# Feed-forward experts ahead of multi-query attention: last slots with tokens stationary, scatters ahead of gathers, first queries' parts moved up

## The chip, the cores and the metric

The kernel runs on one core of one Trainium2 chip. The metric is the device time of one execution in microseconds. A core has five engines with queues of their own: PE (TensorE; PEld is its weight load), DVE (VectorE), ACT (ScalarE), POOL (GpSimd) and SP (SyncE, which here only issues DMAs). They meet through semaphores written out by hand.

## What is computed

Two layers over x of 8 sequences x 512 tokens x 128 channels: linear attention, a mixture of experts, multi-query attention, a filter, each with a layer norm in front and a residual. The change lies in the experts and in the passage to the attention behind them:

```python
capacity = max(1, int(Sz * CAP_FACTOR / E) + 1)          # 512 * 2 / 8 + 1 = 129
scores = softmax(einsum('bsd,ed->bse', x, router_w))
gate_vals, sel_idx = top_k(swapaxes(scores, 1, 2), capacity)
tokens = x[b_idx, sel_idx]
h = gelu(einsum('becd,edh->bech', tokens, w1) + b1)
y = einsum('bech,ehd->becd', h, w2) + b2
out = zeros_like(x).at[b_idx, sel_idx].add(y * gate_vals[..., None])
```

Each of the 8 experts takes 129 tokens of each sequence. 128 of them fill a tile of 128 partitions; the 129th, the "last slot", makes 64 rows in all (8 sequences x 8 experts), which go a way of their own.

## The kernel before, in words

The experts run in 16 phases p (`PHASES`, L985). Phases 0 to 7 are experts 0 to 7 on sequences 0 to 3 (`FIRST`), phases 8 to 15 the same experts on sequences 4 to 7 (`SECOND`). In a phase the four sequences' 128 rows are gathered by POOL with four indirect DMAs (`pool_moe_gathers`, L1040, into one of four buffers of x_row), transposed on PE (`pe_moe_xT`, L1262), copied by ACT, multiplied by w1 in four chunks (`pe_moe_hidden`, L1270, with ACT's Gelu behind each), multiplied by w2 (`pe_moe_output`, L1278) and given bias and gate on DVE (`dve_moe_gated`, L1073, into one of two buffers of yg). The result is added into x. For sequence 0 (`BY_PE`) PE does this with a matmul against a 0/1 mask (`pe_moe_scatter`, L1288). For the others POOL issues an accumulating indirect DMA into x_dram (`pool_moe_scatter`, L1033): three per phase in the first half, four in the second. SP writes x to x_dram before (`x_to_dram`) and reads it back after (`x_from_dram`).

Each engine's order is written out by hand. PE goes through places (p, i), i = 0 to 3 (`moe_pe`, L1356): the hidden chunk i of phase p + 1; at i = 0 the transposes of phase p + 2; a share of the attention's first score maxima (from p = 10 on); `pe_moe_side` (L1330), which holds everything else; output i of phase p. DVE's order is `moe_dve` (L1172), ACT's `moe_act` (L1250), POOL's `moe_pool` (L1049). POOL first gathers phases 0 to 3, and then for each p: the gathers for phase p + 4, a wait for the gated rows of p (m_y), the scatters of p. Bias and gate of phase p wait until the scatters of p - 2 have landed; the gathers for phase n wait until the transposes of n - 4 are done.

The last slots use one bank of PSUM ("side") in stages at fixed phases (`LAST_AT`, L1010): transpose of the 64 gathered rows (p = 1), hidden layer with the weights stationary and 8 columns moving (p = 2, L1317), output likewise (p = 4, L1323), transpose back (p = 5, L1326). Then `pe_moe_rest` (L1298) spreads them over the tokens, one sequence per place of phases 6 and 7, 64 rows deep (L1300). ACT keeps the result for sequences 1 to 3, DVE adds it into x for 4 to 7, and for sequence 0 PE adds it to the sums.

The passage: when the first half is done, sequence 0 gets its layer norm (statistics on DVE, L305, L310; square root and normalising on ACT), its queries (L2057) and keys (L2064), in the side work of phases 8 to 11. The queries are split into three bf16 parts (`dve_q_parts`, L1690; the first part on ACT), and SP writes these with 18 DMAs per sequence into qT. Sequences 1 to 3 come back from x_dram, get the rest added (L1138) and their statistics, ahead of the split. The attention's maxima, its shift rows (SP, L2024) and its first scores end the passage; POOL's causal masking (L1872) of the attention is queued behind POOL's last scatter.

Of the kernel before, what the change touches and what calls it, by code (L numbers as in the profile page):

```python
# [21 lines left out]
P = 128  # L22
# [26 lines left out]
def build(nc, x_in, w_qkv, w_out, router_w, w1, b1, w2, b2, w_attn, w_proj, wf_re, wf_im, f_bias,  # L49
# [18 lines left out]
    with ExitStack() as ctx:  # L68
# [743 lines left out]
        new_stage()  # L812
        rmax = scratch("rmax", [P, B * NT])
# [30 lines left out]
        place = scratch("place", [P, 2, T])  # L844
# [136 lines left out]
        FIRST, SECOND = tuple(range(G)), tuple(range(G, B))  # L981
        BY_PE, DMA_FIRST, DMA_SECOND = FIRST[:1], FIRST[1:], SECOND
        BY_DMA = DMA_FIRST + DMA_SECOND
        SEQ = FIRST + SECOND
# [7 lines left out]
        m_full, m_taken = count("side_bank_filled"), count("side_bank_emptied")  # L992
# [6 lines left out]
        side = bank[0]  # L999
# [3 lines left out]
        def placed_no(e, b):  # L1003
# [5 lines left out]
        LAST_XT, LAST_HIDDEN, LAST_OUTPUT, LAST_T = range(4)  # L1009
        LAST_AT = {1: LAST_XT, 2: LAST_HIDDEN, 4: LAST_OUTPUT, 5: LAST_T}  # L1010
        REST_AT = dict(zip(((6, 0), (6, 1), (6, 2), (6, 3), (7, 0), (7, 1), (7, 2)), BY_DMA))
        REST_SUM_AT = dict(zip(((7, 3),), BY_PE))
        fill_no = {key: n + 1 for n, key in enumerate([("last", n) for n in LAST_AT.values()]
                                                      + [("rest", b) for b in BY_DMA])}

# [32 lines left out]

        def moe_pool(pool):  # L1049
# [9 lines left out]
            for p in range(PHASES):  # L1059
                if p + 4 < PHASES:  # L1060
# [39 lines left out]
        def dve_moe_add_sums(dve, b):  # L1100
            dve.wait_ge(m_placed, placed_no(E - 1, b))
            nc.vector.tensor_tensor(x_sb[:, b], x_sb[:, b], sums[b][:, :].rearrange("p (k d) -> p k d", d=D),
                                    ALU.add).then_inc(m_added, 1)

        def dve_moe_last(dve, stage_no):
            by_seq = seqmask[0:BE, :].unsqueeze(2).broadcast_to([BE, B, D])
            dve.wait_ge(m_full, fill_no["last", stage_no])
# [1249 lines left out]
```

## Time and profile before

| | us |
|---|---|
| median of 3 runs | 752.31 |
| lowest and highest | 749.36, 752.98 |
| the profiled execution's own time | 752.71 |
| its span, first to last instruction | 751.0 |
| PE busy | 618.1 (82%) |
| DVE busy | 521.4 (69%) |
| POOL busy | 391.2 (52%) |
| ACT busy | 374.9 (50%) |

Rows of the trace give a start in us, a duration, an engine, a line of the kernel, an operation and what it writes and reads; [..] is the engine's idle time just before, and what ended it. The experts' phases run from about 250 to 434 us of the span, the attention's eight turns follow. An f32 matmul shows as two PE instructions. Matmuls are pipelined, so their durations overlap; the chain of waits gives them without the overlap.

### The profile page before, as it was taken

How to read it: one execution, taken by the hardware profiler on the slowest of the kernel's cores; microseconds unless marked ns; L12 is line 12 of the kernel's file. 1: busy time of each engine (PE TensorE's matmuls, PEld its weight loads, DVE VectorE, ACT ScalarE, POOL GpSimd, SP SyncE). 2: the span in 40 equal slices, each digit the busy share in tenths (PEclk: the TensorE clock that was granted, in tenths of full speed). 3: DMA queues.
4: the chain of work that ended last, by engine and by line, in shares of the span. 5: the costliest groups of instructions: out<-in, count | busy, mean ns of one | idle time of the engine just before them, and what ended most of it. 6: DMA issues, size and time to landing. Idle time of an engine off the chain costs nothing.

```text
span 751.0 us, 14209 instructions
## 1 busy us (share of the span) xinstructions
PE 618.1 (82%) x4111; PEld 369.9 (49%) x4111; DVE 521.4 (69%) x1779; ACT 374.9 (50%) x800; POOL 391.2 (52%) x529
## 2 busy tenths in 40 slices
PE   2478888888405999999799778999999999999894
PEld 1235555554302688776566533545454545444453
DVE  8458888887794112225478859898989898987554
ACT  0322333331450423326622357777777777767873
POOL 0077777776004777776887554343434343433341
PEclk9989999999855999999999989999999999999997
DMA  9400000000040122244663244040304030200011
GB/s 297 133 0 1 1 0 0 0 1 0 16 140 28 49 43 39 39 93 84 110 98 35 26 82 53 10 59 10 59 10 60 9 60 9 60 5 2 24 52 42
DMA packets 45145, 34.55 MB, mean 46 GB/s; under 512 B 4304, under 2 KB 41728, under 8 KB 45072
## 3 DMA queue, kind: packets, MB, share of 16 engines
q1 hardware_dynamic: 33584, 25.15, 14.5%
q0 software_dynamic: 10144, 7.90, 7.5%
q10 hardware_dynamic: 1344, 0.62, 0.3%
q8 instruction: 34, 0.56, 0.3%
q14 instruction: 39, 0.32, 0.2%
HBM read 14.13 MB, written 9.70 MB: 32 GB/s over the span
## 4 chain that ended last, share of the span: by engine, by line
PE 46%; DVE 16%; issue 8%; ACT 4%; POOL 1%; DMA 1%; DVEq 0%; ACTq 0%; POOLq 0%
PE bank L2146 8%; PE wide L1275 6%; DVE masked L1744 6%; PE wide L2133 5%; PE wide L2082 5%; PE wide L1283 4%; PE bank L1283 4%; PE bank L2082 2%; PE wide L2158 2%; ACT L282 1%; DVE mx L1744 1%; DVE slot_t L886 1%; POOL x_row L1045 1%; PE bank L2057 1%; PE bank L1300 1%
## 5 line engine op out<-in xcount | busy, mean ns | idle before, releaser
L1941 ACT ACTIVATE pexp<-wide 128x512 f32<-128x512 f32 (+2 forms) x384 | 180.9, 536 | 77.9 <-PE wide L2133 75.9
L1744 DVE CUSTOM_DVE_ANT_0 masked<-wide,mask_qk 128x128 f32<-128x128 f32 (+3 forms) x423 | 182.8, 477 | 46.9 <-PE wide L2082 46.1
L1872 POOL TENSOR_SCALAR_AFFINE_SELECT pexp<-pexp 128x256 f32<-128x256 f32 x256 | 106.4, 429 | 166.7 <-ACT pexp L1941 165.2
L2133 PE MATMUL wide<-qT,kTe 128*128 128x256 bf16 (+3 forms) x512 | 121.8, 301 | 6.1 <-ACT pexp L1941 3.7
L2082 PE MATMUL wide<-kTm,qT 128*128 128x128 bf16 (+3 forms) x423 | 102.6, 300 | 13.2 <-DVE mx L1744 10.8
L1036 POOL DMA_INDIRECT x_dram<-yg,row_u x56 | 89.4, 1597 | 30.6 <-DVE yg L1088 15.7
L1225 ACT ACTIVATE hT<-wide,b1T 128x512 f32<-128x512 f32 x64 | 43.9, 686 | 100.7 <-PE wide L1275 100.7
L1045 POOL DMA_INDIRECT x_row<-xln_dram,row_u x64 | 62.6, 978 | 52.5 <-DVE slot_tok L915 33.6
L2146 PE MATMUL bank<-pexp,vx 128*32 128x512 f32 (+3 forms) x1024 | 85.4, 446 | 4.9 <-POOL pexp L1872 4.9
L2133 PEld LDWEIGHTS wide<-qT,kTe 128*128 128x128 bf16 x512 | 48.6, 99 | 42.5 <-ACT pexp L1941 23.1
L1275 PE MATMUL wide<-xgT,w_sb 128*128 128x512 f32 x128 | 67.4, 612 | 1.5 <-ACT xgT L1218 1.5
L2082 PEld LDWEIGHTS wide<-kTm,qT 128*128 128x128 bf16 x423 | 35.7, 97 | 65.8 <-DVE mx L1744 48.3
L615 POOL TENSOR_TENSOR kv<-kx,qv 128x1024 f32<-128x1024 f32 x32 | 62.0, 1949 | 1.1 <-PE wide L718 1.1
L2146 PEld LDWEIGHTS bank<-pexp,vx 128*32 128x32 f32 x1024 | 26.2, 110 | 45.5 <-issue 27.7
L1744 DVE CUSTOM_DVE_ANT_0 masked<-bank,mask_qk 128x256 f32<-128x256 f32 (+3 forms) x89 | 45.5, 528 | 4.0 <-PE bank L2082 4.0
L409 DVE TENSOR_TENSOR prod<-wide,qs 128x1024 f32<-128x1024 f32 x26 | 31.7, 1224 | 21.3 <-PE wide L718 20.2
L717 PE MATMUL wide<-kv,cst 128*128 128x512 f32 x64 | 35.9, 645 | 11.5 <-DVE prod L409 5.6
L1744 DVE DVE_READ_ACCUMULATOR2_ANT mx<- 128x1 f32 x512 | 42.5, 83 | 0.0
L421 DVE TENSOR_REDUCE y_in<-prod 128x128 f32<-128x1024 f32 x32 | 38.2, 1213 | 1.3 <-PE bank L741 0.6
L1283 PE MATMUL wide<-w_sb,hT 128*128 128x128 f32 x256 | 34.9, 280 | 0.0
L1283 PEld LDWEIGHTS wide<-w_sb,hT 128*128 128x128 f32 x256 | 32.1, 192 | 5.2 <-issue 4.3
L1283 PE MATMUL bank<-w_sb,hT 128*128 128x128 f32 x256 | 34.6, 279 | 0.0
(282 smaller groups left out, 1046.6 us busy)
## 6 DMA issues: line engine op xcount, KB each, us to landing
qT<-qp SPq DMA_DIRECT2D x126, 64.0 KB
x_sb<-in_L_attn_x SPq DMA_DIRECT2D x8, 256.0 KB, 6.7
w_sb<-in_L_ffn_w SPq DMA_DIRECT2D x1, 2048.0 KB, 13.1
xln_dram<-hT SPq DMA_DIRECT2D x8, 256.0 KB, 2.3
x_dram<-x_sb SPq DMA_DIRECT2D x7, 256.0 KB, 2.7
x_sb<-x_dram SPq DMA_DIRECT2D x7, 256.0 KB, 3.1
out_x<-x_sb SPq DMA_DIRECT2D x7, 256.0 KB, 2.3
qT<-qp_first SPq DMA_DIRECT2D x18, 64.0 KB
```

Source lines behind the costliest of these rows:

```text
L615: nc.gpsimd.tensor_tensor(kv[:, k % 2, :].rearrange("p (h m l) -> p h m l", l=L, m=L), kx[:, par, k, :].rearrange("p (h l) -> p h l", l=L) ...
L1036: nc.gpsimd.indirect_dma_start(out=x_dram, out_offset=bass.IndirectOffsetOnAxis(ap=row_u[:, b * E + e:b * E + e + 1], axis=0), in_=yg[:, e ...
L1045: nc.gpsimd.indirect_dma_start(out=x_row[:, p % 4, j, :], out_offset=None, in_=xln_dram, in_offset=bass.IndirectOffsetOnAxis(ap=row_u[:, a ...
L1225: nc.scalar.activation(hT[:, q % 2, c, :], psH[c % 2], ACT.Gelu, bias=b1T[:, e * HC + c:e * HC + c + 1]).then_inc(m_h, 1)
L1275: nc.tensor.matmul(psH[c % 2], w1_sb[:, p % E, c * P:(c + 1) * P], xgT[:, p % 2, :], start=True, stop=True).then_inc(m_hp, 1)
L1283: ins = nc.tensor.matmul(psYe[p % 2][:, j * D:(j + 1) * D], hT[:, p % 2, c, j * P:(j + 1) * P], w2_sb[:, p % E, c, :], start=c == 0, stop= ...
L1744: ins = nc.vector.tensor_tensor_reduce(out=masked[:, n % 4, at], in0=bank_of(n)[:, at], in1=mask_qk[:, T - w:T], scale=1.0, scalar=LEAST, ...
L1872: nc.gpsimd.affine_select(out=pexp[:, at, :, 0:P], in_=pexp[:, at, :, 0:P], pattern=[[0, 2], [1, P]], compare_op=ALU.is_ge, fill=0.0, base ...
L1941: nc.scalar.activation(pexp[:, exp_slot(b, 2 * step + h // 2), h % 2:h % 2 + nh, 0:w], scores_bank(b, m)[:, 0:nh * w].rearrange("p (h t) - ...
L2082: ins = nc.tensor.matmul(place[:, hh * w:(hh + 1) * w], qT[:, b % QB, h + hh, k * P:(k + 1) * P], kTm[:, b % 2, 0:w], start=True, stop=True)
L2133: ins = nc.tensor.matmul(scores_bank(b, m)[:, hh * w:(hh + 1) * w], kTe[:, par, j * P:(j + 1) * P], qT[:, b % QB, 4 * qd + h + hh, j * P:T ...
L2146: ins = nc.tensor.matmul(psO[32 * g:32 * g + 32, j * P:T], vx[:, b % 2, j, :], pexp[:, exp_slot(b, 2 * step + g // 2), g % 2, 0:w], start= ...
```

## The change

Four edits in the experts' phases, with their buffers and semaphores:

- **Last slots.** The hidden layer now takes the tokens as the stationary side, padded from 8 to 32 columns per expert, in four strips of 32 columns of the array with w1 moving (8 matmuls of 512 columns, phase 2). DVE copies the two banks out; PE transposes them back in 8 transposes (phase 3, a new stage). The output has the 8 tokens' hidden columns stationary and w2 moving, four strips (32 matmuls of 128 columns, phase 4). SP puts the rows in order with eight small DMAs (no transpose at phase 5).
- **Rest.** One fill per tile of 128 tokens, all four in phase 6: two matmuls of 32 rows and 512 columns, one for sequences 0 to 3 into bank 0, kept by ACT, one for 4 to 7 into bank 6, added into x by DVE. Sequence 0's share is added by DVE in phase 7, no longer by PE.
- **POOL.** For p = 4 to 11 the scatters of p stand ahead of the gathers for p + 4. For p = 0 to 3 the order is as before.
- **Passage.** DVE's splitting of the first queries stands behind sequence 1 and ahead of sequences 2 and 3 (the third and fourth).

SP writes the second half's x to DRAM only after the last fold, no longer one after each.

```diff
+            sp.wait_ge(m_taken, LAST_FILLS)
+            for g in range(G):
+                for j in range(E // G):
+                    sp.dma_start(y_last[j * G + g:BE:E, :], yl_rows[32 * g:32 * g + B, j * D:(j + 1) * D]).then_inc(m_yr, 16)
+            sp.wait_ge(m_taken, LAST_FILLS + NT)
             for b in DMA_SECOND:
-                sp.wait_ge(m_taken, fill_no["rest", b])
                 x_to_dram(sp, b, 1)
             for b in DMA_FIRST:
                 x_from_dram(sp, b)
...
             for p in range(PHASES):
-                if p + 4 < PHASES:
+                if p < SCATTERS_LEAD:
                     pool_moe_gathers(pool, p + 4)
                 pool.wait_ge(m_y, p + 1)
                 if p == E:
@@ -1065,6 +1070,8 @@
                 for b in half_of(p):
                     if b in BY_DMA:
                         pool_moe_scatter(pool, p % E, b)
+                if SCATTERS_LEAD <= p < PHASES - 4:
+                    pool_moe_gathers(pool, p + 4)
                 if p == E + 1:
                     pool_v(pool, 0, 0)
...
             if stage_no == LAST_XT:
-                nc.vector.tensor_copy(xlT[:, :], side[:, 0:BE]).then_inc(m_taken, 1)
+                dve.wait_ge(m_xz, 1)
+                nc.vector.tensor_copy(xlT[:, :, 0:B], side[0][:, 0:BE].rearrange("p (b e) -> p e b", e=E)).then_inc(m_taken, 1)
             elif stage_no == LAST_HIDDEN:
-                nc.vector.tensor_tensor(
-                    hl_in[:, :, :, :].rearrange("p e c b -> p (e c) b"),
-                    side[:, 0:E * HC * B].rearrange("p (n b) -> p n b", b=B),
-                    b1T[:, :].unsqueeze(2).broadcast_to([P, E * HC, B]), ALU.add).then_inc(m_taken, 1)
+                nc.vector.tensor_copy(h_last[:, 0, :], side[0][:, :])
+                nc.vector.tensor_copy(h_last[:, 1, :], side[1][:, :]).then_inc(m_taken, 1)
+            elif stage_no == LAST_HT:
+                for j in range(E // G):
+                    ins = nc.vector.tensor_tensor(
+                        hl_in[:, j * G:(j + 1) * G, :, :].rearrange("p g c b -> p c g b"),
+                        side[j][:, :].rearrange("p (c g r) -> p c g r", g=G, r=32)[:, :, :, 0:B],
+                        b1T[:, j * G * HC:(j + 1) * G * HC].rearrange("p (g c) -> p c g", c=HC).unsqueeze(3)
+                        .broadcast_to([P, HC, G, B]), ALU.add)
+                ins.then_inc(m_taken, 1)
             elif stage_no == LAST_OUTPUT:
-                nc.vector.tensor_tensor(ylT[:, :, :].rearrange("p b e -> p e b"),
-                                        side[:, 0:BE].rearrange("p (e b) -> p e b", b=B),
-                                        b2T[:, :].unsqueeze(2).broadcast_to([P, E, B]), ALU.add).then_inc(m_taken, 1)
+                for g in range(G):
+                    rows = slice(32 * g, 32 * g + B)
+                    ins = nc.vector.tensor_tensor(yl_rows[rows, :].rearrange("b (j d) -> b j d", d=D),
+                                                  side[0][rows, 0:E // G * D].rearrange("b (j d) -> b j d", d=D),
+                                                  b2rep[rows, g::G, :], ALU.add)
+                ins.then_inc(m_taken, 1)
             else:
-                nc.vector.tensor_tensor(rest_r[0:BE, :, :], side[0:BE, 0:D].unsqueeze(1).broadcast_to([BE, B, D]),
-                                        by_seq, ALU.mult).then_inc(m_taken, 1)
-
-        def dve_moe_fold_rest(dve, b):
-
-            dve.wait_ge(m_full, fill_no["rest", b])
-            nc.vector.tensor_tensor(x_sb[:, b], x_sb[:, b], side[:, :].rearrange("p (k d) -> p k d", d=D),
+                dve.wait_ge(m_yr, 16 * E)
+                nc.vector.tensor_tensor(rest_r[0:BE, :, :], y_last.unsqueeze(1).broadcast_to([BE, B, D]),
+                                        by_seq, ALU.mult).then_inc(m_rr, 1)
...
+        def dve_moe_fold_rest(dve, k):
+
+            dve.wait_ge(m_full, LAST_FILLS + k + 1)
+            nc.vector.tensor_tensor(x_sb[:, G:B, k, :], x_sb[:, G:B, k, :], side[1][:, :].rearrange("p (b d) -> p b d", d=D),
                                     ALU.add).then_inc(m_taken, 1)
 
-        def act_moe_keep_rest(act, b):
-
-            act.wait_ge(m_full, fill_no["rest", b])
-            nc.scalar.activation(masked[:, DMA_FIRST.index(b), :], side[:, :], ACT.Copy).then_inc(m_taken, 1)
+        def act_moe_keep_rest(act, k):
+
+            act.wait_ge(m_full, LAST_FILLS + k + 1)
+            nc.scalar.activation(masked[:, k, :], side[0][:, :], ACT.Copy).then_inc(m_kept, 1)
+
+        def dve_moe_first_rest(dve):
+            dve.wait_ge(m_kept, NT)
+            nc.vector.tensor_tensor(x_sb[:, 0], x_sb[:, 0], masked[:, :, 0:D], ALU.add).then_inc(m_first, 1)
...
-                if (p, 0) in REST_AT and REST_AT[p, 0] in DMA_SECOND:
-                    dve_moe_fold_rest(dve, REST_AT[p, 0])
+                if p == 0:
+                    nc.vector.memset(xlT[:, :, :], 0.0).then_inc(m_xz, 1)
                 for b in BY_PE:
                     dve_moe_place(dve, p, b)
                 if p in LAST_AT:
                     dve_moe_last(dve, LAST_AT[p])
-                for i in range(1, G):
-                    if (p, i) in REST_AT and REST_AT[p, i] in DMA_SECOND:
-                        dve_moe_fold_rest(dve, REST_AT[p, i])
+                if p == REST_P:
+                    for k in range(NT):
+                        dve_moe_fold_rest(dve, k)
+                if p == REST_P + 1:
+                    dve_moe_first_rest(dve)
                 dve_moe_gated(dve, p)
...
-            for n in range(1, G):
+            dve_moe_add_rest(dve, SEQ[1])
+            dve_moe_stats(dve, 1)
+            dve_q_parts(dve, 0, range(1, SPLITS))
+            for n in range(2, G):
                 dve_moe_add_rest(dve, SEQ[n])
                 dve_moe_stats(dve, n)
             dve_var_eps(dve, ln3, 1, G)
-            dve_q_parts(dve, 0, range(1, SPLITS))
             dve_moe_gated(dve, E + 1)
...
-        def pe_moe_rest(b, into, start, stop):
-            for k in range(NT):
-                ins = nc.tensor.matmul(into[:, k * D:(k + 1) * D], rest_l[:, k * P:(k + 1) * P],
-                                       rest_r[:, b, :], start=start, stop=stop)
-            return ins
-
-        def pe_moe_last(pe, stage_no, i):
-
-            if fill_no["last", stage_no] > 1:
-                pe.wait_ge(m_taken, fill_no["last", stage_no] - 1)
-            two = range(E // G * i, E // G * (i + 1))
-            ins = None
-            if stage_no == LAST_XT and i == G - 1:
+        def pe_moe_rest(pe, k):
+
+            pe.wait_ge(r_last.sem, r_last.total(1))
+            pe.wait_ge(m_rr, 1)
+            pe.wait_ge(m_taken, LAST_FILLS + k)
+            pe.wait_ge(m_kept, k)
+            for half in range(2):
+                rows = slice(32 * half, 32 * half + 32)
+                ins = nc.tensor.matmul(side[half][:, :], rest_l[rows, k * P:(k + 1) * P],
+                                       rest_r[rows, G * half:G * half + G, :].rearrange("r b d -> r (b d)"),
+                                       start=True, stop=True)
+            ins.then_inc(m_full, 1)
+
+        def pe_moe_last(pe, stage_no, j):
+
+            pe.wait_ge(m_taken, stage_no)
+            if stage_no == LAST_XT:
+                if j == 0:
+                    return
                 pe.wait_ge(m_lg, 16)
-                ins = nc.tensor.transpose(side[:, 0:BE], x_last[:, :], ident[0:BE, 0:BE])
+                ins = nc.tensor.transpose(side[0][:, 0:BE], x_last[:, :], ident[0:BE, 0:BE])
             elif stage_no == LAST_HIDDEN:
-                for e in two:
-                    for c in range(HC):
-                        at = (e * HC + c) * B
-                        ins = nc.tensor.matmul(side[:, at:at + B], w1_sb[:, e, c * P:(c + 1) * P],
-                                               xlT[:, :].rearrange("p (b e) -> p e b", e=E)[:, e, :], start=True, stop=True)
-            elif stage_no == LAST_OUTPUT:
+                for g in range(G):
+                    ins = nc.tensor.matmul(side[j][32 * g:32 * g + 32, :], xlT[:, j * G + g, :], w1_sb[:, j * G + g, :],
+                                           start=True, stop=True)
+            elif stage_no == LAST_HT:
+                for c in range(HC):
+                    ins = nc.tensor.transpose(side[j][:, c * P:(c + 1) * P], h_last[:, j, c * P:(c + 1) * P], ident)
+            else:
                 pe.wait_ge(m_lh, 1)
-                for e in two:
-                    for c in range(HC):
-                        ins = nc.tensor.matmul(side[:, e * B:(e + 1) * B], w2_sb[:, e, c, :], hl[:, e, c, :],
+                for c in range(HC):
+                    for g in range(G):
+                        e = j * G + g
+                        ins = nc.tensor.matmul(side[0][32 * g:32 * g + B, j * D:(j + 1) * D], hl[:, e, c, :], w2_sb[:, e, c, :],
                                                start=c == 0, stop=c == HC - 1)
-            elif stage_no == LAST_T and i == G - 1:
-                ins = nc.tensor.transpose(side[0:BE, 0:D], ylT[:, :, :].rearrange("p b e -> p (b e)"), ident)
-            if i == G - 1:
+            if j:
                 ins.then_inc(m_full, 1)
 
         def pe_moe_side(pe, p, i):
             if 0 < p <= E and 0 < i <= len(BY_PE):
                 pe_moe_scatter(pe, p - 1, BY_PE[i - 1])
-            if p in LAST_AT:
-                pe_moe_last(pe, LAST_AT[p], i)
-            if (p, i) in REST_AT:
-                b = REST_AT[p, i]
-                pe.wait_ge(r_last.sem, r_last.total(1))
-                pe.wait_ge(m_taken, fill_no["rest", b] - 1)
-                pe_moe_rest(b, side, True, True).then_inc(m_full, 1)
-            if (p, i) in REST_SUM_AT:
-                b = REST_SUM_AT[p, i]
-                pe_moe_rest(b, sums[b], False, False)
+            if p in LAST_AT and LAST_AT[p] < LAST_ROWS and i in (1, 2):
+                pe_moe_last(pe, LAST_AT[p], i - 1)
+            if p == REST_P:
+                pe_moe_rest(pe, i)
             if (p, i) in XT_AT_P:
                 if XT_AT_P[p, i] == 0:
-                    pe.wait_ge(m_taken, len(fill_no))
+                    pe.wait_ge(m_taken, LAST_FILLS + NT)
+                    pe.wait_ge(m_kept, NT)
                 pe_xT(pe, XT_AT_P[p, i], first=True)
```

## Rows read from the trace of the kernel before

**Rows 1.** Windows: us, then busy time of each engine, PEclk, DMA share, GB/s

```profile
250.00:342.00 92.00, 92.00 (x614) 73.24 (x613) 21.37 (x37) 28.97 (x46) 68.62 (x58) 1.00 0.31 53
342.00:434.00 92.00, 77.74 (x474) 53.45 (x472) 65.57 (x264) 41.68 (x75) 69.82 (x52) 1.00 0.49 71
...
437.40:440.60 3.20, 3.19 (x17) 0.64 (x18) 0.00 (x0) 0.00 (x0) 2.06 (x6) 0.50 0.55 114
```

**Rows 2.** Timeline of POOL: gathers (L1045) and scatters (L1036)

```profile
259.64 1.62 POOL L1036 DMA_INDIRECT x_dram<-yg,row_u  x1 [0.30 <-issue]
...
265.30 1.02 POOL L1045 DMA_INDIRECT x_row<-xln_dram,row_u  x1 [0.30 <-issue]
...
269.15 0.94 POOL L1045 DMA_INDIRECT x_row<-xln_dram,row_u  x1 [0.30 <-issue]
...
341.60 1.62 POOL L1036 DMA_INDIRECT x_dram<-yg,row_u  x1 [2.92 <-DVE yg L1088]
...
435.00 1.56 POOL L1036 DMA_INDIRECT x_dram<-yg,row_u  x1 [0.30 <-issue]
```

**Rows 3.** One line, L1045: from a gather's issue to its landing

```profile
DMA to landing us min/median/max: 2.4/2.5/6.3
```

**Rows 4.** Chain of waits, phases 1 to 8: start, us, engine, tile, line, count

```profile
266.47 1.69 PE bank L1317 x16
...
282.85 0.86 PE wide L1275 x2
283.71 0.89 PE wide L1293 x8
284.61 0.89 PE bank L1283 x8
...
301.81 1.69 PE bank L1323 x16
...
314.24 1.09 PE bank L1300 x8
...
337.69 1.09 PE wide L1300 x8
...
340.73 0.44 PE wide L1267 x4
```

**Rows 5.** Timeline of PE: passage, then first values' matmuls of the attention (L2146)

```profile
352.85 0.63 PE L2051 MATMUL bank<-cst,xln 128*128 128x128 f32 x4 [1.59 <-ACT xln L1897]
...
374.13 0.60 PE L1267 MATMUL wide<-cst,x_row 128*128 128x128 f32 x4
...
397.31 0.60 PE L1267 MATMUL wide<-cst,x_row 128*128 128x128 f32 x4
...
437.41 3.21 PE L2146 MATMUL bank<-pexp,vx 128*32 128x512 f32 x16 [4.46 <-POOL pexp L1872]
...
454.03 0.86 PE L2146 MATMUL bank<-pexp,vx 128*32 128x256 f32 x16
...
459.90 1.71 PE L2146 MATMUL bank<-pexp,vx 128*32 128x512 f32 x16
```

**Rows 6.** Timeline of DVE: gates (L1088), additions (L1138), first queries' split (L1688)

```profile
265.94 0.69 DVE L1088 TENSOR_TENSOR yg<-yg,gate 128x512 f32<-128x512 f32 x1
...
352.05 0.66 DVE L1138 TENSOR_TENSOR x_sb<-x_sb,masked 128x512 f32<-128x512 f32 x1
...
354.09 0.66 DVE L1138 TENSOR_TENSOR x_sb<-x_sb,masked 128x512 f32<-128x512 f32 x1
...
356.75 0.69 DVE L1688 TENSOR_TENSOR q_rest<-bank,qp_first 128x512 f32<-128x512 f32 x1 [0.34 <-ACT qp_first L1911]
...
360.39 0.71 DVE L1088 TENSOR_TENSOR yg<-yg,gate 128x512 f32<-128x512 f32 x1
...
386.68 0.70 DVE L1088 TENSOR_TENSOR yg<-yg,gate 128x512 f32<-128x512 f32 x1
```

**Rows 7.** Timeline of SP's queue: six small DMAs

```profile
423.70 4.25 SPq L2024 DMA_DIRECT2D qT<-mT  x6
```

More of the change, by code:

```diff
@@ L812, in build @@
         new_stage()
+        FIRST, SECOND = tuple(range(G)), tuple(range(G, B))
+        BY_PE, DMA_FIRST, DMA_SECOND = FIRST[:1], FIRST[1:], SECOND
+        BY_DMA = DMA_FIRST + DMA_SECOND
+        SEQ = FIRST + SECOND
         rmax = scratch("rmax", [P, B * NT])
@@ L843, in build @@
         tokens_f = scratch("tokens_f", [P, T])
-        place = scratch("place", [P, 2, T])
+        place = scratch("place", [P, len(BY_PE), T])
         qp_first = scratch("qp_first", [P, PARTS, T], BF16)
@@ L976, in route_sync @@
                 sp.dma_start(of_sequence(xln_dram, b), rx[:, b]).then_inc(r_xd, 16)
[L981 to L984, printed above, removed]
         PHASES = 2 * E
@@ L998, in build @@
         psX, psH, psYe = bank[5], (wide[:, 0:512], wide[:, 512:1024]), (bank[2], bank[7])
-        side = bank[0]
+        side = (bank[0], bank[6])
         sums = dict(zip(BY_PE, (bank[1],)))
@@ L1005, in placed_no @@
             return len(BY_PE) * e + BY_PE.index(b) + 1
[L1009 to L1014, printed above, removed]
+        LAST_XT, LAST_HIDDEN, LAST_HT, LAST_OUTPUT, LAST_ROWS = range(5)
+        LAST_AT = {1: LAST_XT, 2: LAST_HIDDEN, 3: LAST_HT, 4: LAST_OUTPUT, 5: LAST_ROWS}
+        REST_P, LAST_FILLS = 6, 4
         def x_to_dram(sp, b, half):
@@ L1106, in dve_moe_last @@
             by_seq = seqmask[0:BE, :].unsqueeze(2).broadcast_to([BE, B, D])
-            dve.wait_ge(m_full, fill_no["last", stage_no])
+            if stage_no < LAST_ROWS:
+                dve.wait_ge(m_full, stage_no + 1)
             if stage_no == LAST_XT:
-                nc.vector.tensor_copy(xlT[:, :], side[:, 0:BE]).then_inc(m_taken, 1)
+                dve.wait_ge(m_xz, 1)
+                nc.vector.tensor_copy(xlT[:, :, 0:B], side[0][:, 0:BE].rearrange("p (b e) -> p e b", e=E)).then_inc(m_taken, 1)
@@ L1134, in dve_moe_add_rest @@
         def dve_moe_add_rest(dve, b):
-            i = DMA_FIRST.index(b)
             dve.wait_ge(m_back[b], 16)
-            dve.wait_ge(m_taken, fill_no["rest", b])
-            nc.vector.tensor_tensor(x_sb[:, b], x_sb[:, b], masked[:, i, :].rearrange("p (k d) -> p k d", d=D),
-                                    ALU.add).then_inc(m_done, 1)
+            dve.wait_ge(m_kept, NT)
+            nc.vector.tensor_tensor(x_sb[:, b], x_sb[:, b], masked[:, :, b * D:(b + 1) * D], ALU.add).then_inc(m_done, 1)
@@ L1228, in act_moe_aside @@
         def act_moe_aside(act, p, i):
-            if p in LAST_AT and LAST_AT[p] == LAST_HIDDEN and i == G - 1:
-                act.wait_ge(m_taken, fill_no["last", LAST_HIDDEN])
+            if p in LAST_AT and LAST_AT[p] == LAST_HT and i == G - 1:
+                act.wait_ge(m_taken, LAST_HT + 1)
                 nc.scalar.activation(hl[:, :, :, :], hl_in[:, :, :, :], ACT.Gelu).then_inc(m_lh, 1)
-            if (p, i) in REST_AT and REST_AT[p, i] in DMA_FIRST:
-                act_moe_keep_rest(act, REST_AT[p, i])
+            if p == REST_P:
+                act_moe_keep_rest(act, i)
             if (p, i) in XT_AT_P:
```

11 lines of the change are left out of this document (8 added, 3 removed).

## Prediction

> **What bounds the kernel now.** I read the windows first. From 250 to 342 us (phases 0 to 7, the first four sequences) PE is busy in all 92 us, and DVE and ACT in less than a third of them; from 342 to 434 us (phases 8 to 15) PE has 14 us of gaps [rows 1]. So time taken off PE in the first half looks like a gain. Then I read POOL's timeline, because POOL is busy for 69 us of each half and every expert's rows go in and out by it. In the table I call y(p) the moment at which phase p's gated rows are ready on DVE, S(p) the scatters that POOL then issues, G(n) the four gathers for phase n, and X(n) PE's transposes of these, which stand near the start of phase n-2. Three scatters take 259.64 to 265.30, 5.66 us, so four (second half) about 7.55; four gathers take 265.30 to 270.39, 5.1 us [rows 2]. The last gather is issued 3.85 us into its block [rows 2] and lands 2.5 us after that [rows 3]: **a gather block needs 6.35 us from its start to its data.** POOL's own need is therefore 10.8 us per phase in the first half and 12.6 in the second. The old order hides this: G(p+4) is issued before POOL waits for y(p), so at S(7) POOL had already issued G(11) and waited 2.92 us for DVE [rows 2]. What ends the passage is POOL's last scatter at 435.00 [rows 2]: the first values' matmul waits for POOL behind it, 4.46 us [rows 5]. Everything later follows that.
>
> **PE's part.** Removed: eight bursts of 1.69 us (16 instructions each, weight loads for 8 columns; four of L1317, four of L1323) and eight of 1.09 us (L1300), together 22.2 us, all on PE's path [rows 4]. Added:
> - Hidden layer: 8 matmuls in strips of 32 columns, four over 512 columns per place. The nearest rows are the values' matmuls, which already run four strips: 1.71 us for two steps of four matmuls, of 512 and 384 columns by the code [rows 5], so 1.71 x 512/896 = 0.98 per place, 2.0 in all. One after another they would cost 0.86 each [rows 4], 6.9.
> - Eight transposes: 2 x 0.44 [rows 4] = 0.9.
> - Output: 32 matmuls over 128 columns, four strips. The two steps of 256 and 128 columns took 0.86 [rows 5], so 0.29 per 128 columns, 8 x 0.29 = 2.3. One after another: 32 x 0.22 = 7.1 (0.89 per four [rows 4]).
> - Rest: 4 x 2 matmuls, each on 32 rows and 512 columns. No row shows two row strips side by side. Bounds: 0.98 for a pair that overlaps like the column strips, 1.72 (2 x 0.86) for one that doesn't [rows 4, 5]. I take 0.98, 3.9 in all, because the strips of rows 5 are nearest; one by one adds 3.0. The Trainium skill, TensorE: Matmul & The Clock Gate, Part 3 (Packing small matmuls), states that matmuls on different 32-row groups run at once, which would give the lower bound; no row here shows it.
> - A new wait: the second rest fill waits for DVE's first fold, which now stands behind the place mask, and that waits for PE's own scatter at this place. Two DVE operations of 512 columns at most 0.69 each [rows 6]: 1.4 us, with PE's outputs queued behind it. Below nothing it cannot be.
>
> PE's work falls from 22.2 to 10.5 us.
>
> **What else is added lies beside this.** DVE gets two copies of 512 columns, six small additions, a zeroing and one more residual addition, ACT one more copy; in this half both are busy under a third of the time [rows 1]. If that cover were gone, the two copies would cost 1.4. SP gets eight small row copies, 0.71 us of issue each (six took 4.25 [rows 7]), 5.7 us plus landing; with y(4) as below they are done about 302.5, and the rest matmuls that need them come at 310. The four writes of x on SP now wait for the last fold, but S(8) asks for them 20 us later.
>
> **POOL's part: where the gain goes.** From p = 4 the order is S(p), then G(p+4). G(p+4) can no longer start before y(p), and so X(p+4) comes no sooner than 0.3 + 5.66 + 6.35 = 12.3 us after y(p) in the first half, 14.2 in the second. PE asks for X(p+4) right after y(p+1), and a plain phase is 4 x (0.89 + 0.86) + 0.89 + 0.44 = 8.33 us [rows 4]. The lead over PE is lost. Step by step, bias and gate being 1.4 us:
> - y(1) is 266.63 as before [rows 6]; y(2) = 276.9, y(3) = 286.1, y(4) = 296.8 (8.33 plus the added work).
> - POOL runs without a pause from 259.64: S(0), G(5), S(1), G(6), S(2), G(7), S(3), S(4) end at 303.2 (five scatter and three gather blocks, 5 x 5.66 + 3 x 5.1 = 43.6). G(8) lands at 309.6. PE wants X(8) at 304.5 and **waits 5.0 us**.
> - y(6) = 309.6 + 0.44 + 4 x 0.98 + 4 x 0.89 + 3 x 0.86 + 0.89 + 1.4 + 1.4 = 323.8. POOL, free at 319.1 after S(5) and G(9), waits 5. S(6) 324.1, G(10) 329.8, S(7) 334.9 (341.60 before [rows 2]), G(11) 340.6, landed 347.0.
> - X(10) = 336.1, 4.5 us late; y(8) = 345.0. X(11) = 347.0.
>
> Phase 9 holds the other move. The first queries' transposes come 0.44 + 0.89 + 0.86 = 2.2 us after X(11), at 349.2, and DVE's splitting 3.9 us after these (352.85 to 356.75 [rows 5, 6]), 353.1. Before, DVE reached the splitting only 0.34 us ahead of ACT [rows 6], so the move gains at most 0.34. What it costs: the additions and statistics of sequences three and four, 2.04 each [rows 6], were done in DVE's waiting time and now come after the split (1.9) and ahead of the gate: 353.1 + 1.9 + 4.1 + 0.2 + 1.4 = 360.7 = y(9), against 361.1 before. Behind that gate are the first keys, and POOL's S(9). SP's 18 query copies, which follow ACT's part, start neither earlier nor later by this.
> - S(9) 361.0, G(13) 368.6 (POOL's small copy behind S(9) is left out), X(13) = 374.9 (374.13 before [rows 5]). From X(13) to y(11) took 13.2 [rows 5, 6]: y(11) = 388.1.
> - S(11) 388.4, G(15) 395.9, **X(15) = 402.3 against 397.31 before** [rows 5]: +5.0.
>
> No gather follows, PE works in order, so +5.0 reaches the last scatter and the end. The attention keeps its length.
>
> **TensorE's clock.** After the 4.46 us wait, 16 values' instructions took 3.21 us against 1.71 [rows 5], with a granted clock of 0.50, that is 1.2 instead of 2.4 GHz [rows 1]. Each new wait of that length costs 1.5 us or nothing. I charge the one at X(8), which delays S(7) and all behind it, and half of one at X(15) (PE waits some 4 us there): +2. A second charge at X(15) is the upper end; X(10) and X(13) are absorbed by POOL's next lateness.
>
> **Sum.** +5.0 + 2.0 = +7.0, less an estimated 1.0 of PE's 14 us of gaps [rows 1] that fall into the new stalls: +6. The profiled execution took 752.71 (span 751.0), 0.4 above the median 752.31; 752.7 + 6 = **758.7**.
>
> **Rivals.**
> - POOL never pauses (the faster side). Place: y(6), y(9), y(11) come before POOL is free. Then G(15) ends at 259.64 + 8 x 5.66 + 4 x 7.55 + 11 x 5.1 = 391.2 and lands 1.25 us later, at 392.5, 4.8 us before the old X(15): **747.9**. It decides if y(6) falls below 319, y(9) below 358 and y(11) below 384. For it: only three or four us are missing each time. Against it: X(8) at 309.6 is fixed by POOL alone. A gain of the whole 11.7 us of PE is ruled out by this same sum. 0.10.
> - Gain and loss cancel: no fold wait (-1.4), the clock stays at 2.4 GHz (-2), PE's and DVE's waits after X(13) and X(15) are swallowed (-1.5): +1, **753.7**. For it: many waits of a tenth to one us stand there now. 0.22.
> - The strips do not do what the edit says and run one after another: 6.9 + 7.1 + 6.9 instead of 2.0 + 2.3 + 3.9. y(4) is then 306.5, close to the old value, y(6) about 336 and S(7) about 347, 12 later than above: +18, **771**. Overlap lost in the rest alone: +3, 762. Against it: the rows of the values' matmuls. 0.13 for both, mostly the latter.
>
> **How the numbers follow.** My forecast has 0.55. About 0.5% (3.8 us) is what a measurement of this kernel can tell from no change. Slower by more: nearly all of the forecast (0.50) and the last rival (0.13), 0.63. Faster by more: the first rival, 0.10. The remainder, 0.27, is the cancelling case and the forecast's lower edge. The forecast's own range is 755 to 763; ten to twenty per cent outside leaves 750 to 764.
>
> **What would show it.** Right: PE waits of 2 to 5 us at the transposes of the gathered rows (L1267) with the gather's DMA as releaser, in phases 6, 8 and 9 to 13, where now there is none; POOL waiting for y(6), and S(7) near 335; X(15) at 400 to 405; the last scatter later than 435. The strips at 1.0 us per four hidden matmuls. Wrong: POOL without pauses, gathers landed ahead of X(15) before 397, or the gate of phase 9 earlier than 357.

## The result, and the profile after

The changed kernel takes **773.62 us** (median of 4 runs, 772.98 to 774.53) against 752.55 for the kernel before on the same chip: ratio 1.029, 95% interval [1.026, 1.0321]. The forecast was 758.7, with a range of 750 to 764. The direction was right, and the size was 15 us too small. The profiled execution took 772.98, its span is 771.2, 20.2 longer than before.

Line numbers move: the transposes of gathered rows are now L1293 (L1267 before), gathers L1048, scatters L1039, the gate L1095, hidden chunks L1301, outputs L1309, sequence 0's matmuls against the mask L1319, the rest L1332 and VectorE's fold of it L1146, the first queries' split L1715, key slots L2099, first score maxima L2109, SP's query copies L2044.

Windows of the changed kernel, with the columns of [rows 1]: the two halves, then the six us behind each of four waits.

```profile
250.00:342.00 92.00, 80.24 (x514) 55.53 (x515) 24.47 (x44) 29.48 (x46) 66.70 (x54) 0.96 0.30 51
342.00:434.00 92.00, 73.30 (x398) 52.73 (x399) 49.64 (x196) 33.88 (x58) 61.30 (x49) 0.88 0.44 68
311.20:317.50 6.30, 6.24 (x18) 3.65 (x19) 0.00 (x0) 1.20 (x2) 5.08 (x5) 0.53 0.39 39
341.90:348.00 6.10, 6.10 (x24) 5.07 (x25) 0.00 (x0) 1.28 (x2) 4.88 (x5) 0.52 0.61 86
372.30:379.00 6.70, 6.65 (x27) 5.52 (x28) 0.00 (x0) 2.63 (x6) 5.19 (x5) 0.53 0.63 111
404.70:410.00 5.30, 5.30 (x21) 4.11 (x22) 2.03 (x10) 0.67 (x2) 4.08 (x5) 0.57 0.34 40
```

Before, PE had no gap in the first half, and PEclk was 1.00 in both [rows 1]. Now there are gaps in both, and in four stretches the granted clock is near 0.5, 1.2 instead of 2.4 GHz. What precedes each is in the timeline of PE:

```profile
311.26 1.11 PE L1293 MATMUL wide<-cst,x_row 128*128 128x128 f32 x4 [5.76 <-DMA x_row<-xln_dram,row_u]
312.31 1.22 PE L1332 MATMUL bank<-rest_r,rest_l 32*128 32x512 f32 x1
312.31 1.22 PE L1332 MATMUL wide<-rest_r,rest_l 32*128 32x512 f32 x1
...
319.93 0.66 PE L1332 MATMUL bank<-rest_r,rest_l 32*128 32x512 f32 x1 [1.37 <-DVE x_sb L1146]
...
341.88 1.11 PE L1293 MATMUL wide<-cst,x_row 128*128 128x128 f32 x4 [4.52 <-DMA x_row<-xln_dram,row_u]
...
372.35 1.11 PE L1293 MATMUL wide<-cst,x_row 128*128 128x128 f32 x4 [7.65 <-DMA x_row<-xln_dram,row_u]
...
404.70 1.11 PE L1293 MATMUL wide<-cst,x_row 128*128 128x128 f32 x4 [6.20 <-DMA x_row<-xln_dram,row_u]
...
416.61 0.60 PE L1293 MATMUL wide<-cst,x_row 128*128 128x128 f32 x4
```

The four with a DMA as releaser are X(8), X(10), X(12) and X(14): 24.1 us of waiting for gathered rows, where the kernel before waited for none. POOL's timeline shows the other side:

```profile
308.69 0.95 POOL L1048 DMA_INDIRECT x_row<-xln_dram,row_u  x1 [0.30 <-issue]
...
329.89 1.62 POOL L1039 DMA_INDIRECT x_dram<-yg,row_u  x1 [9.44 <-DVE yg L1095]
...
340.69 1.61 POOL L1039 DMA_INDIRECT x_dram<-yg,row_u  x1 [0.30 <-issue]
...
365.88 0.94 POOL L1048 DMA_INDIRECT x_row<-xln_dram,row_u  x1 [0.30 <-issue]
...
397.68 0.94 POOL L1048 DMA_INDIRECT x_row<-xln_dram,row_u  x1 [0.30 <-issue]
...
454.26 1.55 POOL L1039 DMA_INDIRECT x_dram<-yg,row_u  x1 [0.30 <-issue]
```

POOL stands 9.44 us ahead of S(6), with G(10) behind that wait; PE in turn stands for G(10). The two wait for each other by turns. The last scatter comes at 454.26, 19.3 us after that of before [rows 2], which is nearly all of the span's 20.2. X(15), the last row above, is late by the same 19.3 us (416.61 against 397.31 [rows 5]): nearly the whole loss lies ahead of it.

### The profile page after: what moved, and what is told of

It is laid out like the page before. It is cut to its first block, busy times and chain, and to the rows that moved or that the text cites. A ratio compares the mean times of both kernels' runs of the same rounds, so it can differ in the third digit from the quotient of the medians.

```text
span 771.2 us, 14051 instructions
## 1 busy us (share of the span) xinstructions
PE 615.9 (80%) x4022; PEld 358.8 (47%) x4022; DVE 524.9 (68%) x1787; ACT 376.2 (49%) x801; POOL 392.3 (51%) x529
## 4 chain that ended last, share of the span: by engine, by line
PE 34%; DVE 15%; POOL 10%; issue 9%; DMA 4%; ACT 2%; SPq 1%; DVEq 0%; ACTq 0%; POOLq 0%
PE bank L2173 8%; POOL x_row L1048 5%; DVE masked L1771 5%; POOL x_dram L1039 5%; PE wide L2160 5%; PE wide L2109 4%; PE wide L1309 3%; DMA x_row<-xln_dram,row_u 3%; PE wide L1301 2%; PE bank L2109 2%; PE wide L2185 2%; SPq L2044 1%; DVE mx L1771 1%; DVE slot_t L890 1%; DVE slot_v L888 1%
## 5 line engine op out<-in xcount | busy, mean ns | idle before, releaser
L1039 POOL DMA_INDIRECT x_dram<-yg,row_u x56 | 88.9, 1587 | 49.0 <-DVE yg L1095 34.5
L2109 PE MATMUL wide<-kTm,qT 128*128 128x128 bf16 (+3 forms) x423 | 102.3, 299 | 11.1 <-DVE mx L1771 10.3
L1048 POOL DMA_INDIRECT x_row<-xln_dram,row_u x64 | 63.2, 988 | 52.7 <-DVE slot_tok L919 33.5
L1301 PE MATMUL wide<-xgT,w_sb 128*128 128x512 f32 x128 | 70.0, 633 | 1.5 <-ACT xgT L1244 1.5
L2109 PEld LDWEIGHTS wide<-kTm,qT 128*128 128x128 bf16 x423 | 35.9, 98 | 63.7 <-DVE mx L1771 48.0
L1309 PEld LDWEIGHTS wide<-w_sb,hT 128*128 128x128 f32 x256 | 36.4, 213 | 12.2 <-issue 9.2
L1309 PE MATMUL wide<-w_sb,hT 128*128 128x128 f32 x256 | 38.8, 300 | 0.0
L1293 PE MATMUL wide<-cst,x_row 128*128 128x128 f32 x64 | 12.2, 324 | 28.4 <-DMA x_row<-xln_dram,row_u 28.4
```

Of the source, the lines that this page charges most:

```text
L1039: nc.gpsimd.indirect_dma_start(out=x_dram, out_offset=bass.IndirectOffsetOnAxis(ap=row_u[:, b * E + e:b * E + e + 1], axis=0), in_=yg[:, e ...
L1048: nc.gpsimd.indirect_dma_start(out=x_row[:, p % 4, j, :], out_offset=None, in_=xln_dram, in_offset=bass.IndirectOffsetOnAxis(ap=row_u[:, a ...
L1301: nc.tensor.matmul(psH[c % 2], w1_sb[:, p % E, c * P:(c + 1) * P], xgT[:, p % 2, :], start=True, stop=True).then_inc(m_hp, 1)
L1309: ins = nc.tensor.matmul(psYe[p % 2][:, j * D:(j + 1) * D], hT[:, p % 2, c, j * P:(j + 1) * P], w2_sb[:, p % E, c, :], start=c == 0, stop= ...
L2109: ins = nc.tensor.matmul(place[:, hh * w:(hh + 1) * w], qT[:, b % QB, h + hh, k * P:(k + 1) * P], kTm[:, b % 2, 0:w], start=True, stop=True)
```

## The experiments

Theory: the loss comes from the gathers that stand behind the scatters, and what each late gather costs is made of its wait, the halved clock behind it, and a slower landing while query copies are in flight. Rivals: the last slots or the passage cost the time themselves. All ratios are to the kernel before, on the same chip.

### Gathers ahead again, the rest as changed

```diff
-        SCATTERS_LEAD = 4
+        SCATTERS_LEAD = 12
```

> The changed kernel with the gathers ahead of the scatters at every p, as in the kernel before; the last slots with the tokens stationary and the passage order of the changed kernel stay. Theory: the loss comes from the gathers that stand behind the scatters, so with them ahead again TensorE has no wait for gathered rows (24.3 us in the changed kernel), its clock stays up after 311 us, and the 11.7 us of its work that the last slots give back remain: 738 to 746 us. Rival: the last slots or the passage cost the time by themselves, and the gathers only show it: 752 us or more.

744.84 us, ratio 0.9909 [0.9874, 0.9945]: the theory holds, and this version beats both kernels. Its waits of PE from 262 to 460 us (what waited, for what; us in total, times, longest):

```profile
PE wide L2109 <- DVE mx L1771: 7.0, 12, 1.9
PE bank L2099 <- DVE kx L1702: 5.4, 2, 4.6
...
PE wide L1293 <- DMA x_row<-xln_dram,row_u: 0.2, 1, 0.2
```

The waits for rows are gone. So one decision about the order on POOL costs 0.038 of 752, some **29 us**, and the last slots give back some 7. The prediction's sum takes 11.7 us off PE, with the fold wait of 1.4 already counted in, so some 5 do not arrive. The profile shows a longer wait for the first key slots, 4.58 us instead of 1.83 in the kernel before, and a low granted clock behind it (0.54):

```profile
354.10:360.00 5.90, 5.89 (x23) 4.73 (x24) 0.00 (x0) 2.28 (x5) 4.55 (x5) 0.54 0.76 131
```

That this wait is what holds the 5 us back is not shown: the last experiment shortens it, and nothing is gained.

### The last slots alone

The run above, and in the passage:

```diff
-            dve_moe_add_rest(dve, SEQ[1])
-            dve_moe_stats(dve, 1)
-            dve_q_parts(dve, 0, range(1, SPLITS))
-            for n in range(2, G):
+            for n in range(1, G):
                 dve_moe_add_rest(dve, SEQ[n])
                 dve_moe_stats(dve, n)
             dve_var_eps(dve, ln3, 1, G)
+            dve_q_parts(dve, 0, range(1, SPLITS))
```

> The run above with the passage in the order of the kernel before as well, so that of the change the last slots alone are left. Theory: the move of the first queries' parts costs y(9) some 3 us by VectorE's wait for the first part on ScalarE, so this one is up to 3 us faster than the run above, about 736 to 743 us. Rival: the move pays, since the query copies start earlier: 1 to 3 us slower than the run above.

746.17 us, 0.9927 [0.9886, 0.9969]. Its interval overlaps that of the run above: the effect of the passage cannot be told from nothing. Neither expectation is shown.

### The order on POOL alone, in the kernel before

```diff
-                if p + 4 < PHASES:
+                if p < 4:
                     pool_moe_gathers(pool, p + 4)
...
                         pool_moe_scatter(pool, p % E, b)
+                if 4 <= p < PHASES - 4:
+                    pool_moe_gathers(pool, p + 4)
```

> The kernel before with only the order on GpSimd changed: from p = 4 on the scatters of p stand ahead of the gathers of p + 4. Theory: this alone makes TensorE wait for gathered rows at phases 8, 10, 12 and 14, with its clock halved after each, so it is slower than the kernel before by 15 to 25 us: 767 to 778 us. Rival: the slower last slots of the kernel before leave the scatters early enough, or the waits need the other parts of the change: 752 to 756 us.

775.98 us, 1.034 [1.0318, 1.0362]. This one edit reproduces the loss without the others. Its profiled execution was its quickest (768.37), so its rows understate it; its waits of PE still begin with

```profile
PE wide L1269 <- DMA x_row<-xln_dram,row_u: 15.7, 5, 4.6
```

They stand ahead of X(8), X(11), X(12), X(14) and, for half a microsecond, X(15). The expectation had X(10) and not X(11): the order alone does not fix which phases wait, and the loss comes all the same.

With the four kernels together, the order costs 0.034 with the old last slots and 0.038 with the new ones.

### The passage undone in the changed kernel

The edit of the second experiment, with the scatters ahead.

> The changed kernel with the passage in the order of the kernel before; last slots and order on GpSimd stay as changed. Theory: y(9) comes some 3 us earlier, and with it the scatters and gathers behind it: 768 to 772 us. Rival: the even phases set the end and y(9) is of the odd ones, so nothing moves: 773 to 774 us; or the move paid and its undoing costs 1 to 3 us.

772.56 us, 1.0283 [1.025, 1.0315]: no difference that shows from the changed kernel's 1.029, and not the 768 to 772 of the theory. The move neither pays nor costs anything that shows, though VectorE's timeline has its price in the changed kernel:

```profile
360.97 0.69 DVE L1715 TENSOR_TENSOR q_rest<-bank,qp_first 128x512 f32<-128x512 f32 x1 [4.56 <-ACT qp_first L1938]
...
367.81 0.69 DVE L1095 TENSOR_TENSOR yg<-yg,gate 128x512 f32<-128x512 f32 x1
```

VectorE waits 4.56 us for ScalarE's part before it goes on to sequences three and four and to this gate, y(9) at 368.5. Without the move, y(9) is 3.6 us earlier counted from X(10) (23.0 us after it instead of 26.6), but X(12) only 0.5 (30.0 instead of 30.5): G(12) stands behind S(8), not behind y(9).

### Spare work through the waits

```diff
+                    if i == 0 and p in FILLERS:
+                        pe.wait_ge(m_taken, LAST_FILLS + (NT if p >= E else 0))
+                        for n in range(FILLERS[p]):
+                            nc.tensor.matmul(bank[6], ident, w1_sb[:, n, :], start=True, stop=True)
                     if i == 0 and p + 2 < PHASES:
                         pe_moe_xT(pe, p + 2)
...
+        FILLERS = {6: 5, 8: 4, 10: 6, 12: 5}
```

> The changed kernel with 5, 4, 6 and 5 spare matmuls (identity by 512 columns of the first weights, 0.86 us each at full clock, into a free bank) on TensorE just ahead of the transposes of phases 8, 10, 12 and 14, so that it works through the waits for gathered rows. Theory: each of those waits also costs the clock, which the rows show at 0.52 to 0.57 for some 6 us after each; without that, work behind each wait is 2 to 4 us shorter, and 760 to 768 us come out. Rival: the wait for the rows sets the time alone, and the work behind it has room: 772 to 775 us; or the spare work itself delays: above 775 us.

766.03 us, 1.0192 [1.013, 1.0253]. **Twenty useless matmuls made the kernel about 7 us faster** (0.0098 x 752). The two intervals only just part, but the run of the next section, on the same chip and without the spare work, took 774.65. The timeline of PE, the windows behind three of the waits, and one that follows the first:

```profile
309.70 0.66 PE L1293 MATMUL wide<-cst,x_row 128*128 128x128 f32 x4 [1.37 <-DMA x_row<-xln_dram,row_u]
...
339.26 0.66 PE L1293 MATMUL wide<-cst,x_row 128*128 128x128 f32 x4 [1.14 <-DMA x_row<-xln_dram,row_u]
...
367.73 0.66 PE L1293 MATMUL wide<-cst,x_row 128*128 128x128 f32 x4 [2.73 <-DMA x_row<-xln_dram,row_u]
```

```profile
309.00:315.00 6.00, 4.55 (x26) 2.96 (x26) 0.71 (x2) 1.88 (x3) 5.08 (x4) 1.00 0.38 34
317.00:323.00 6.00, 6.00 (x24) 2.87 (x22) 1.16 (x2) 1.67 (x3) 1.58 (x2) 0.72 0.12 33
339.00:345.00 6.00, 5.74 (x40) 4.78 (x41) 2.11 (x10) 1.93 (x3) 4.78 (x5) 1.00 0.60 83
367.70:374.00 6.30, 6.27 (x32) 4.55 (x32) 0.00 (x0) 3.10 (x7) 5.13 (x4) 0.73 0.65 116
```

The rows land no earlier after their issue, but the granted clock behind the waits is 1.00, 1.00 and 0.73 instead of 0.53, 0.52 and 0.53, and X(12) comes at 367.73 instead of 372.35. The low clock is not gone altogether: behind the fold wait, from 317 to 323 us, it is granted at 0.72, so the 7 us are a part of what the clock costs.

### Query copies held until phase 14 is transposed

```diff
             q_rows(sp, 0, 1)
+            sp.wait_ge(m_xgp, 15)
             q_rows(sp, 1, 0)
```

> The changed kernel with the second sequence's 18 query copies on SyncE's queue held back until the transposes of phase 14 are done. Theory: the gathers of phase 14 land late because these copies are in flight (6.9 us from the last issue, where the others take 2.5); with them gone, the wait ahead of phase 14 falls from 6.2 to about 2 us, and the time by 4 to 6 us, to 767 to 770 us. Rival: the gathers are late for another reason, such as the scatters in front of them: the wait stays at 6 us, and the time at 773 us; or the copies are then needed by the maxima of the second sequence, and the time does not fall.

774.65 us, 1.0303 [1.0267, 1.034]: the time did not fall, as the second rival had it, but for another reason than a late copy. The last two gather waits of PE, the landing of phase 14's gathers (L1048, 392 to 399 us), then SP's copies and the last gather of phase 15 on POOL:

```profile
398.50 0.66 PE L1293 MATMUL wide<-cst,x_row 128*128 128x128 f32 x4 [1.82 <-DMA x_row<-xln_dram,row_u]
...
418.29 1.12 PE L1293 MATMUL wide<-cst,x_row 128*128 128x128 f32 x4 [9.90 <-DMA x_row<-xln_dram,row_u]
```

```profile
DMA to landing us min/median/max: 2.5/2.5/2.6
```

```profile
399.19 12.09 SPq L2044 DMA_DIRECT2D qT<-qp  x18
```

```profile
409.82 0.94 POOL L1048 DMA_INDIRECT x_row<-xln_dram,row_u  x1 [0.30 <-issue]
```

The wait ahead of X(14) fell from 6.20 to 1.82 us, as the theory said, and its gathers landed in 2.5; the copies then ran from 399 to 411 us over the gathers of phase 15, the last of which landed 8.5 us after its issue (409.82 to 418.29). The delay went where the copies went.

### Copies held until phase 15 is transposed, alone and with the spare work

The same line with 16 in place of 15; the second kernel has the fillers too.

> The changed kernel with the second sequence's query copies held until the transposes of phase 15, the last ones, are done. With a hold until phase 14 the wait ahead of 14 fell from 6.2 to 1.8 us and a wait of 9.9 us appeared ahead of phase 15, whose gathers then met the copies. Theory: no gather of the last two phases meets a copy now, both waits are gone but for 2 us, and the time is 765 to 769 us. Rival: the copies, 12 to 13 us long from about 410 us, come too late for the second sequence's maxima: 771 us or more.

> The run above with the spare matmuls of the filler run as well. Theory: clock and late landing are separate costs, so the two gains add up: 7.6 us of the filler and 4 to 8 us of the held copies, 757 to 763 us. Rival: both shorten the same wait, and together they give no more than the better of the two: 764 us or more.

Alone: 769.8 us, 1.0222 [1.0205, 1.0239], so 0.0068, some 5 us, faster than the changed kernel. The total is a little above the theory's 765 to 769, and a wait of 4.00 us ahead of X(15) stayed (the first of these rows is X(14)):

```profile
399.72 0.66 PE L1293 MATMUL wide<-cst,x_row 128*128 128x128 f32 x4 [1.70 <-DMA x_row<-xln_dram,row_u]
...
413.60 1.11 PE L1293 MATMUL wide<-cst,x_row 128*128 128x128 f32 x4 [4.00 <-DMA x_row<-xln_dram,row_u]
```

That wait is no slow landing: the last gather ahead of it was issued at 411.04, 2.56 us earlier; POOL, busy without a pause since 385.82, came to it late.

With the spare work: 762.79 us, 1.0111 [1.0067, 1.0156], 0.0179 or some 13 us faster. That is the sum of the two gains (7 and 5), as the theory had it: clock and landing look like separate costs. It is not shown beyond doubt, since two of the four runs lie above the rival's 764, and the interval overlaps that of the spare work alone.

### The swap in one half alone

```diff
-        SCATTERS_LEAD = 4
+        SCATTERS_LEAD = range(4, 8)
...
-                if p < SCATTERS_LEAD:
+                if p < PHASES - 4 and p not in SCATTERS_LEAD:
...
-                if SCATTERS_LEAD <= p < PHASES - 4:
+                if p in SCATTERS_LEAD:
```

and, for the second kernel, `range(8, 12)`.

> The changed kernel with the scatters ahead of the gathers at p = 4 to 7 alone, and the gathers ahead again from p = 8. Theory: each wait for rows costs by itself, and the lead comes back once the gathers stand ahead: the waits of phases 8 and 10 stay (10 us together, and 2 to 4 us more for the clock), those of 12 and 14 go: 754 to 761 us. Rival: a lead once lost is not won back, because the scatters that were issued late now delay: 768 us or more.

> The changed kernel with the scatters ahead at p = 8 to 11 alone. Theory: only the waits of phases 12 and 14 appear, lengthened by the query copies (7.7 and 6.2 us in the changed kernel, somewhat less here since the phases ahead leave some lead), and 4 to 6 us for the clock: 755 to 764 us. Rival: the waits of phases 8 and 10 start a chain that these belong to, and without it the lead holds: 745 to 749 us.

First half: 760.29 us, 1.0119 [1.0097, 1.014]; second: 758.76 us, 1.0093 [1.0062, 1.0123]. Against the kernel with the gathers ahead throughout (0.9909) that is 0.021 and 0.018, together 0.039, and both halves at once cost 0.038: the prices of the two halves add up, and the lead comes back where the old order returns. PE's gather waits, first half:

```profile
309.83 1.12 PE L1293 MATMUL wide<-cst,x_row 128*128 128x128 f32 x4 [5.85 <-DMA x_row<-xln_dram,row_u]
...
342.92 1.11 PE L1293 MATMUL wide<-cst,x_row 128*128 128x128 f32 x4 [4.54 <-DMA x_row<-xln_dram,row_u]
```

and second half:

```profile
356.17 1.12 PE L1293 MATMUL wide<-cst,x_row 128*128 128x128 f32 x4 [11.01 <-DMA x_row<-xln_dram,row_u]
...
389.06 1.11 PE L1293 MATMUL wide<-cst,x_row 128*128 128x128 f32 x4 [6.79 <-DMA x_row<-xln_dram,row_u]
```

The expectation that X(12) and X(14) would wait less there than in the changed kernel was wrong: they wait more, 11.01 and 6.79 us. The lead of the first half is PE's, not POOL's: POOL stands without a pause there, with seven scatters from 331.91 to 345.34 ahead of G(12).

### An attempt to gain more

Gathers ahead; the first keys' parts and slots between sequences three and four on VectorE, ScalarE's root one step later:

```diff
             for n in range(2, G):
                 dve_moe_add_rest(dve, SEQ[n])
                 dve_moe_stats(dve, n)
+                if n == 2:
+                    dve_k_parts(dve, 0)
+                    dve_k_slots(dve, 0)
...
-            dve_k_parts(dve, 0)
-            dve_k_slots(dve, 0)
...
-        STD_AT = {0: (E, G - 1), 1: (E + 1, G - 1)}
+        STD_AT = {0: (E, G - 1), 1: (E + 2, 0)}
```

> The kernel with the gathers ahead, last slots and passage as changed, and in the passage two more moves: the first keys' parts and slots on VectorE between sequences three and four, and ScalarE's root for those sequences one step later, behind the next Gelu. Theory: without the moves TensorE waits 4.6 us for the key slots (4.58 us, L1702) and works at half clock behind it for some 5 us; with them the wait falls to 1.5 us or less and the clock stays up: 738 to 742 us. Rival: the later root delays the second sequence's normalised rows, or TensorE waits for a Gelu in the same place: 744 us or more.

744.17 us, 0.989 [0.9874, 0.9907], the same as without the moves (0.9909): the theory's 738 to 742 did not come. The wait for the key slots fell from 4.58 to 1.22 us, and others took its place (waits of PE from 262 to 460 us):

```profile
PE bank L2100 <- DVE kx L1703: 2.1, 2, 1.2
PE wide L1294 <- DMA x_row<-xln_dram,row_u: 2.0, 2, 1.2
PE wide L2110 <- issue: 1.9, 1, 1.9
```

## Why the prediction was right in direction and wrong in size

**The cause was right.** It put the loss on G(p+4) starting no sooner than S(p), and this edit alone gives 1.034 in the kernel before, while its removal from the changed kernel gives 0.9909. The first rival, POOL never pausing (747.9), fell with the wait of 9.44 us ahead of S(6). So did the case in which gain and loss cancel: the fold wait came, and the clock went down.

**PE's part was right.** Four hidden or sixteen output matmuls in strips take 0.99 us (269.53 to 270.52, 289.47 to 290.46) where 0.98 per place and 1.15 were forecast. The two row strips of the rest start in the same instant (both at 312.31), and a pair takes 1.05 us at full clock (0.62 and 0.42 in the chain of waits), forecast 0.98. The Trainium skill, TensorE: Matmul & The Clock Gate, Part 3 (Packing small matmuls), states that different 32-row groups run at once; the trace agrees. The fold wait is 1.37 us, forecast 1.4. The rival whose strips run one after another gave 771, near the time measured, and its mechanism is nowhere in the trace: a time that fits is no evidence for a cause.

**The passage** was put at no gain and no loss, and none shows in either pair of runs.

**X(8) was nearly right**: 309.6 with 5.0 of waiting forecast, 311.26 with 5.76 measured. The wait ahead of X(10) too: 4.5 and 4.52, though it came 5.8 us late (341.88, forecast 336.1), and S(7) with it (340.69, forecast 334.9). The steps after each of the two failed.

**Failed step 1: the price of the clock.** "Each new wait of that length costs 1.5 us or nothing", 2 us in all. The chain of waits of the changed kernel behind X(8) (start, us, what):

```profile
311.26 1.11 PE wide L1293 x4
312.38 1.15 PE bank L1332
...
313.53 0.85 PE bank L1332
...
314.39 2.00 PE wide L1309 x8
316.39 1.27 PE wide L1301 x2
317.66 0.91 PE wide L1319 x8
```

These take 7.31 us (311.26 to 318.57). At full clock they are 0.44, 1.05, 0.89, 0.86 and 0.89, together 4.13 [rows 4, and the pair above]. So this wait costs 3.2 us behind it, twice the figure taken from the values' matmuls [rows 5]; with the spare work ahead of it the same chain took 4.57 us (309.70 to 314.27), 2.7 less. Behind X(10) it is much the same: 12.0 us from there to y(8), where 8.9 were forecast. The forecast's 1.5 was the slowdown of one group, and the window that the prediction shows ends with the group [rows 1]; the next one in the kernel before, which it did not use, shows the granted clock still at 0.64:

```profile
440.60:444.00 3.40, 3.28 (x18) 2.08 (x15) 2.87 (x14) 1.58 (x4) 0.81 (x2) 0.64 0.23 69
```

In the changed kernel the four stretches shown at the low clock are 5.3 to 6.7 us long, and all of PE's work in them takes longer. And the clock falls at four waits, where one and a half were charged: y(6) came at 329.61 (forecast 323.8), y(8) at 353.88 (345.0). The spare work recovers some 7 us. The Trainium skill, TensorE: Matmul & The Clock Gate, Part 1 (HAM oscillation — how this bites in real kernels), describes a kernel whose every stage starts at the low clock after its DMA wait and pays each time; the four windows at 0.52 to 0.57 agree. The prediction should have charged each wait of its own forecast.

**Failed step 2: the landing of a gather.** The prediction took the median of [rows 3], 2.5 us, for every gather, though the row's maximum is 6.3. Line L1048 of the changed kernel from 360 to 373 us:

```profile
DMA to landing us min/median/max: 4.1/4.2/6.4
```

and SP's copies:

```profile
361.01 12.01 SPq L2044 DMA_DIRECT2D qT<-qp_first  x18
...
384.33 13.09 SPq L2044 DMA_DIRECT2D qT<-qp  x18
```

The gathers of phase 12 stand beside the first 18 copies; the last was issued at 365.88 and its rows used at 372.35. The last gather of phase 14 was issued at the end of the second 18 and took 7.0 us (397.68 to 404.70). In the kernel before the same slow landings were hidden by the lead. The held copies show the cause for phase 14, and what they cost: 5 us. The first 18 copies were held in no run. But in the run with the swap in the first half alone, phase 12's gathers were issued from 352.45 to 357.62, ahead of those copies (from 361.68), and landed in 2.5 to 3.0 us; so the same cause is likely for phase 12. The Trainium skill, DMA: Bandwidth & Descriptors, Queues, rings and completion order, states that each DMA engine takes turns between the queues that it has work for; that fits gathers slowed by copies of another queue, though no run here shows the turns themselves.

**Failed step 3: which phases set the pace.** With y(8) at 345.0 the prediction followed X(11), X(13) and X(15). By its own figures G(12) would have landed about 360 (S(8) at 346.0, plus 7.55 and 6.35), just ahead of y(9) at 360.7, so X(12) cost nothing. With y(8) 9 us later and the landing slow, X(12) was the longest wait, 7.65, and the odd phases had none ahead of 353.12, 385.42 and 416.61 (X(11), X(13), X(15)).

**The sum.** The miss is 773.6 - 758.7 = 14.9 us. Spare work and held copies together take back some 13, of which the forecast had charged 2 for the clock; so about 11 us are steps 1 and 2 with what follows from them. Some 4 us were not taken apart: the clock that the spare work does not win back, phase 12's slow landing, and G(8), which began at 304.82 instead of 303.2, may all have a share. At X(15) PE is already 14.3 us behind the forecast (416.61 against 402.3, to which the clock's 2 were added afterwards).

## What to carry to other kernels

Where one queue both fetches for a later stage and stores for this one, an order that puts the store first ties the fetch to this stage's result and turns a lead of several stages into a loop; compute that loop's length before the work saved elsewhere. Charge each wait of a forecast with the work done at the low clock behind it, and take a landing time from the stretch where it will happen, beside the transfers that will be in flight there, not from a median over the kernel. If a wait cannot be removed, spare matmuls through it can pay.

## What had not been expected of the hardware

Twenty matmuls without use, some 17 us of PE time at 0.86 each, made the kernel 7 us faster, because they lay in waits and the granted clock in the windows behind two of the three shown was 1.00 instead of 0.5. A gather's landing went from 2.5 to 6.4 us, and to 8.5 in one run, beside another queue's copies, and the delay followed the second 18 copies when they were moved.
